# Spacing the row gathers of a four-layer kernel: one weight piece behind each gather in the expert layer, paced gathers and loads in linear attention

## What is computed

```python
x = L0_attn_x
x = _layernorm(x + _L0_attn_ref(x))     # dilated attention on every second row
x = _layernorm(x + _L0_ffn_ref(x, ...)) # switch layer: each row through its best of 8 experts
x = _layernorm(x + _L1_attn_ref(x, W))  # linear attention
x = _layernorm(x + _L1_ffn_ref(x, ...)) # soft mixture: dispatch to 64x32 slots, combine
```

```python
# switch layer, for each expert e; w1[e] is 256 x 2048, w2[e] is 1024 x 256
a, g = jnp.split(x @ w1[e], 2, axis=1)
y = jax.nn.silu(a) * g @ w2[e]
out = jnp.where((max_ind == e)[:, None], y, out)   # then out * max_prob
# linear attention
q, k, v = jnp.split(x @ W, 3, axis=-1)
q, k = elu(q) + 1, elu(k) + 1
V = einsum('bld,bhd,bl->blh', q, einsum('bld,blh->bhd', k, v), 1 / (q . k.sum + EPS))
```

## Time and profile before

| | us |
|---|---|
| median of 3 runs | 1529.8 |
| lowest, highest | 1528.87, 1532.9 |
| profiled execution, its own time | 1531.05 |
| span in the profile (first to last instruction) | 1529.2 |
| outside the span | 1.85 |

### The profile page before, as it was taken

The page is one execution under the profiler, slowest core; times in us unless marked ns, Lnnn a source line. Parts: engine busy times, 40 slices in busy tenths (PEclk is TensorE's granted clock), DMA queues, the critical chain, the costliest instruction groups (busy, mean ns, idle before and its releaser), DMA issues. The chain is left out here.

```text
span 1529.2 us, 27827 instructions
## 1 busy us (share of the span) xinstructions
PE 1380.1 (90%) x8930; PEld 1202.3 (79%) x8931; DVE 885.1 (58%) x1768; ACT 612.1 (40%) x1077; POOL 680.1 (44%) x546
## 2 busy tenths in 40 slices
PE   6997387999999994599978999999999997999997
PEld 3444276888888883477768999999999987999997
DVE  4788612222222223377559877877877853666655
ACT  3554322333333331377643323323323315555553
POOL 6663087776670003411006655655655652540500
PEclk9998688999999997699989999999999998999999
DMA  4112334222220003500023263653653657365350
GB/s 158 45 45 70 124 96 135 97 96 96 96 96 14 14 15 111 195 1 1 1 83 97 84 174 88 178 168 90 179 168 88 179 175 283 129 233 198 137 203 38
DMA packets 109194, 171.17 MB, mean 112 GB/s; under 512 B 6128, under 2 KB 95088, under 8 KB 101712
## 3 DMA queue, kind: packets, MB, share of 16 engines
q1 hardware_dynamic: 100112, 156.00, 31.5%
q0 software_dynamic: 3408, 9.31, 2.1%
q10 hardware_dynamic: 5616, 5.11, 1.0%
HBM read 114.96 MB, written 55.44 MB: 111 GB/s over the span
## 5 line engine op out<-in xcount | busy, mean ns | idle before, releaser
L1572 PE MATMUL disp_psS<-disp_e,last_x 128*128 128x256 f32 x1024 | 233.1, 381 | 3.6 <-POOL disp_e L1659 3.6
L1572 PEld LDWEIGHTS disp_psS<-disp_e,last_x 128*128 128x128 f32 x1024 | 191.2, 191 | 28.2 <-POOL disp_e L1659 4.2
L1557 PE MATMUL disp_psL<-phi_hold,hand_xh 128*128 (+1 forms) x1024 | 200.3, 296 | 4.9 <-DVE disp_e L1724 4.8
L1666 POOL TENSOR_TENSOR disp_s<-disp_e 128x512 f32<-128x512 f32 x64 | 82.3, 1286 | 263.9 <-ACT disp_e L1642 263.9
L1845 PE MATMUL comb_psO<-phi_hold,comb_eh 128*128 (+1 forms) x1024 | 198.2, 291 | 0.4 <-DVE comb_el L1943 0.4
L1557 PEld LDWEIGHTS disp_psL<-phi_hold,hand_xh 128*128 128x128 f32 x1024 | 165.4, 194 | 8.9 <-issue 5.9
L1624 ACT ACTIVATE disp_raw<-disp_psL 128x512 f32<-128x512 f32 x128 | 76.4, 597 | 220.9 <-PE disp_psL L1557 156.4
L1845 PEld LDWEIGHTS comb_psO<-phi_hold,comb_eh 128*128 128x128 f32 x1024 | 156.8, 189 | 0.9 <-DVE comb_el L1943 0.8
L1659 POOL TENSOR_TENSOR disp_e<-disp_e,disp_rs 128x1024 f32<-128x1024 f32 x64 | 151.6, 2369 | 0.0
L1557 PE MATMUL disp_psL<-phi_hold 128*128 (+1 forms) x512 | 145.8, 285 | 0.0
L1845 PE MATMUL comb_psO<-phi_hold,comb_el 128*128 (+1 forms) x512 | 144.1, 281 | 0.0
(11 more groups left out here) (258 smaller groups left out, 3116.1 us busy)
## 6 DMA issues: line engine op xcount, KB each, us to landing
logits<-disp_raw SPq DMA_DIRECT2D x64, 512.0 KB, 4.1
hand_e<-logits SPq DMA_DIRECT2D x32, 1024.0 KB, 6.7
w_raw<-in_w SPq DMA_DIRECT2D x8, 2048.0 KB
disp_wt<-in_w_slot SPq DMA_DIRECT2D x16, 1024.0 KB, 8.0
w_raw<-in_w SPq DMA_DIRECT2D x8, 1024.0 KB
disp_bt<-in_b_slot SPq DMA_DIRECT2D x8, 1024.0 KB, 11.2
slot_y<-disp_yb SPq DMA_DIRECT2D x60, 128.0 KB, 3.2
comb_y_in<-slot_y SPq DMA_DIRECT2D x3, 2048.0 KB, 10.6
```

The costliest lines, as they stand in the source:

```text
L1557: last = nc.tensor.matmul(psL[p][:, b, :], xp[:, kd, t * P:(t + 1) * P], pp[:, kd, bass.ds(k * BLK, BLK)], start=b % 2 == 0 and kd == 0 an ...
L1572: last = nc.tensor.matmul(psS[kd][:, b, :], x[:, b * TB + mc, kd * P:(kd + 1) * P], e[mc % 4][:, b, :], start=mc == 0 and b % 2 == 0, stop ...
L1666: nc.gpsimd.tensor_tensor(s2[:], e[mc % 4][:, 0:2, :], e[mc % 4][:, 2:4, :], ALU.add).then_inc(pair_sum, 1)
```

## The change

In the switch layer the low part of expert 1 is cut into 32 pieces in place of 12: w1's 4096 columns into 16 pieces of 256, w2's 2048 columns into 16 pieces of 128. The loop around it is the same, so one piece now stands behind each gather of slots 3 to 34, and the last four gathers have nothing between them. The semaphore counts stay: `split` goes up by 2 behind the last piece of w1 and by 2 behind the last of w2.

In linear attention the gathers of tiles 0 to 15 stay as they were. Gather t of tiles 16 to 31 waits for `k_raw` to reach t - 15, which is when tile t - 16 has been projected. The first eight low parts of phi stand between gathers 23 and 24, the other eight behind gather 31. On SP, phi's load waits for `k_raw` 2, the load of x of batch 2 for `k_raw` 6, and that of batch 3 for `k_raw` 14.

```diff
-    CHUNK = 512
-    LOW_CHUNKS = (KD * 2 * FF + FK * D) // CHUNK
+    CHUNKS = 16
+    LOW_CHUNKS = 2 * CHUNKS
     def low_chunk(self, pool, e, n):
-        first = KD * 2 * FF // self.CHUNK
-        part, at = (0, n) if n < first else (1, n - first)
+        first = self.CHUNKS
+        part, at = divmod(n, self.CHUNKS)
         _, raw, hi, lo = self.parts()[part]
-        cols = slice(at * self.CHUNK, (at + 1) * self.CHUNK)
+        size = (KD * 2 * FF, FK * D)[part] // self.CHUNKS
+        cols = slice(at * size, (at + 1) * size)
...
             for b in range(B):
-                if b == 2:
-                    sp.dma_start(phi[:], phi_dram.rearrange("(k p) n s -> p k (n s)", p=P)).then_inc(phi_loaded, 16)
                 if b == 1:
                     sp.wait_ge(gathered[TB - 1], 16)
+                if b == 2:
+                    sp.wait_ge(k_raw, 2)
+                    sp.dma_start(phi[:], phi_dram.rearrange("(k p) n s -> p k (n s)", p=P)).then_inc(phi_loaded, 16)
+                if b > 1:
+                    sp.wait_ge(k_raw, (b - 2) * TB + TB - 2)
                 sp.dma_start(x[:, b * TB:(b + 1) * TB, :], rows[:, b * TB:(b + 1) * TB, :]).then_inc(x_loaded[b], 16)
         @block.gpsimd
         def _(pool):
-            for t in range(NT):
+            def fetch(t):
+                wait(pool, k_raw, t - 2 * TB + 1)
                 nc.gpsimd.indirect_dma_start(yg[:, t, :], None, ys_dram, ...
-            for i in range(PARTS):
+
+            def low_part(i):
                 j = i // PARTS_PER_ROW
                 cols = slice(i * PC, (i + 1) * PC)
                 pool.wait_ge(o_raw, j + 1)
                 pool.wait_ge(phi_high, i // (PARTS // KD) + 1)
                 nc.gpsimd.tensor_tensor(lo_flat[:, cols], ...
+
+            for t in range(2 * TB):
+                fetch(t)
+            for b in range(2, B):
+                for t in range(b * TB, (b + 1) * TB):
+                    fetch(t)
+                for i in range((b - 2) * TB, (b - 1) * TB):
+                    low_part(i)
```

## The result

| | before | after |
|---|---|---|
| median of the runs side by side | 1531.08 us | 1505.89 us |
| span in the profile | 1529.2 us | 1502.7 us |

What follows compares the result with a forecast made beforehand. The prediction took PE to bound the kernel, with time to win only where dense POOL gathers stopped it. Gains of 11.0 (switch layer) and 15.5 us (linear attention) made 26.5 off 1529.8: forecast 1503.5 us, range 1499 to 1517.

Steps and rivals of the forecast that it cites:

- PE's holes at 249 and 619 us: Switch layer and linear attention: PE busy only 4.4 of 13 us and 6.5 of 19 us, where time could be won.
- Part 1, the stop: Switch layer, tiles 4 to 15: spacing the gathers 1.86, then 1.58 us apart removes the stop, worth 13.0 us.
- A: Rival: the switch layer's stop stays because gathers 1.6 to 1.9 us apart are too dense; 1514.3 us, chance 0.15 with halves.
- L: Rival: the switch layer's stop stays because the loop's first turn causes it; 1514.3 us, chance 0.05.
- Who stood still: Both stops: ACT stood still first, with waits of 18.6 and 11.6 us that nothing in the engines' records released.
- Part 1, what gets later: Switch layer's expert loads: expert 2 in time by 1 us, PE waits 2 us for expert 3, leaving 11.0 us gained.
- the duration of expert 2's first load: Switch layer: 7.75 us from expert 3's rows, plus 0.7 for four gathers beside it; w1 ready at 273.6.
- Part 2: Linear attention: pacing gathers and loads removes a 16.0 us stop, less 0.5 for phi's load, gaining 15.5 us.
- The model by batch 1's rows: Linear attention, batch 0: without a stop, `lin_kv` follows the second tile's keys by 20.5 us, as in batch 1.
- rival B: Linear attention's stop stays, from sixteen back-to-back gathers with 1 MB of x, or phi's load; 1519 us, chance 0.05.
- what counts is how densely POOL issues gathers: Both stops: gathers 1.25 us apart for long enough stop ACT and slow PE; 2.4 us apart cost nothing.
- Rival C: Both layers: neither stop goes, since bytes in flight count, not spacing; about 1530 us, chance 0.05.

Runs made afterwards that it cites:

- Session C: Follow-up session on another chip without stops, kernel before 1505.4 us: halves of linear attention's pacing, moved burst and thin gathers, each beside the kernel before.
- A: Session of the main result: the whole change against the kernel before, 1505.89 us against 1531.08, ratio 0.9844.
- D: Follow-up session on a chip without stops: the whole change against the kernel before, 1505.31 us against 1505.95, ratio 0.9997; also a moved-burst run.
- the near-zero gap: Kernel before plus a one-column POOL memset (0.1 us) behind each gather of slots 0 to 2 and 15 to 38; 1523.84 us.
- the paced gathers of session C: Kernel before with only linear attention's gathers 16 to 31 paced, loads and switch layer as before; 1505.83 us, ratio 1.0003.
- E: Follow-up session without stops: changed kernel with the next expert's w1 loaded earlier, 1500.86 us against the kernel before's 1505.26; also a moved-burst run.
- B: Follow-up session with stops, kernel before 1530.6 us: switch-layer change only 1521.48 us, linear-attention change only 1512.70, changed kernel with earlier w1 load 1501.22.

## Why the prediction was right, and where it was not

**What stands.** PE's holes at 249 and 619 us were the place of the gain. Each part removed its own stop, and the parts add up (9.1 and 17.9 us alone). Why dense gathers hold PE, and why on some chips or in some sessions only, stays open (below).

**Part 1, the stop.** Forecast: 13.0 us. Gate product 7 comes 13.3 us earlier than before (284.51 to 271.19). Spacing of 1.6 to 1.9 us was enough; the row could not tell, since the choice was made between two ends, and luck has a share in that. Rivals A and L (0.20 together) fell with it. Session C speaks once more against L: the loop's first turn is there, the stop is not.

**Who stood still.** The prediction says that ACT stood still first and that its waits were released by nothing. That reading is wrong: ACT waited for semaphores of PE, raised 16.1 and 15.5 us late (above). The forecast didn't hang on it, since it priced the whole hole and tied it to the gathers. (A small slip beside it: ACT's stop is in step 5, not 6, since the copy at 261.44 is that of tile 3.)

**Part 1, what gets later.** This term was mis-sized. Forecast: expert 2 in time by 1 us, expert 3 late by 2 us. Measured: PE waited at both, and tiles 8 and 11 cost 3.8 and 1.7 us more than in the steady pace. The step that failed is the duration of expert 2's first load. I took 7.75 us from expert 3's rows and added 0.7 for four gathers beside it; it took 10.9 us, with the last gathers and a store beside it (the second weight's 1 MB stood behind expert 3's load too). The loads of 7.6 to 7.8 us without gathers and 10.2 us with them, in the experiments above, point to the gathers. The margin that I had left was 1 us, and w1 was ready 3.1 us later than forecast, at 276.7. A second thing wasn't priced, the clock: at tile 8

```profile
276.90 0.49 PE L922 MATMUL moe_psH<-w_hi,moe_xh 128*128 x1 [1.97 <-POOL w_lo L826]
```

PE waited 2.0 us, and the other 1.8 us are slow matmuls: the granted clock from 278 to 284 us is 0.73, and at 0.50 of it a matmul comes each 0.43 us in place of 0.23. The layer gave 7.7 us up to tile 19 in place of 11. Another 1.5 us came between tile 19 and linear attention. That is not the change: the stretch takes about 194.3 us in some profiles and 195.6 to 195.9 in others, of the same kernel too (the changed one 194.3 in A, 195.7 in D), with no visible cause.

**Part 2.** Forecast: 15.5 us, 16.0 less 0.5 for phi. Measured in the profile: 16.4, and phi was there. The model by batch 1's rows was right to 0.1 us (20.5 and 20.5). One number in the argument against rival B was wrong: behind gather 7 stand 5 MB of loads, not 4 (x of three batches and phi); at its 7.75 us for 2 MB they end at 627, and in the trace they end near 630, still ahead of 637.42.

**The sum** was 26.5 us of span, forecast and measured. That the two agree so closely is luck: the 3.3 us that part 1 gave too little came back as 0.9 in part 2, the 1.5 between the layers that the change didn't cause, and 0.9 of small differences at the start and the end. By the medians it was 25.2.

**What was not foreseen.** The step "what counts is how densely POOL issues gathers" is true only in half. Density is needed: the near-zero gap keeps the stop at 1.25 us, the change loses it at 1.6. It isn't enough: on three chips the same density stops nothing. Something that differs from chip to chip, or from session to session, comes in, and no run here shows what it is.

Three things can be said against guesses. It isn't the program or its data: they are the same. Nor do instruction blocks come late on the queues that the trace records: in the kernel before, blocks are moved at 235 and 244 us, ahead of the stop, and at 615 in linear attention, much as with the paced gathers of session C, at 235, 247 and 606. And what comes late in a stop are first of all semaphores of matmuls that PE had already been through by the profile, which a wait for new instructions would not explain by itself; this is argued, not tested. The Trainium skill, Runtime: NRT & Kernel Launch, section Instruction fetch mechanics, has fetches mostly hidden. The traces of C to E agree, in so far as no semaphore of PE is over 0.02 us late and ACT has no wait put down to "remote"; those of A and B don't show whether the stop has to do with fetching.

One more difference is in the traces, and it leaves a rival untested. Those of A and B lack some 440 to 820 of about 10,280 records of raised semaphores, most of all where the gathers run and most in the kernel before; those of C to E lack hardly any. The stop may come from whatever loses these records, or from the recording itself. Every run here gives its span and clock, so no time is known of an execution that wasn't recorded.

Rival C of the prediction ("neither goes, 1530") was the nearest to a flat outcome, but not its reason: what I never priced is that there might be no stop to remove.

## What to carry to other kernels

An engine that waits for something "remote" may be waiting for its neighbour's late semaphore: look at the engine that should raise it. Read such a stop as a property of that execution until a second chip shows it; run the kernel before beside each experiment, and look at its time first. Long rows of back-to-back indirect DMAs on GpSimd are worth spacing with other work, here to 1.6 us or more apart: it made no measurable difference where nothing stops (ratio 0.9997), and saved 25 us where something does. When a stall is removed, what it covered comes due: re-time the chain behind it (here loads and divisions of weights, 5.5 us) from the changed start, and ask of each load what runs beside it.

## What the runs showed of the hardware that was not expected

- The same kernel takes 1531 us in sessions A and B and 1505 us on the three other chips of C to E, each time stable (all runs of a session within 0.6%). The difference is two stops, worth 13 and 16 us, during bursts of indirect DMAs 1.25 us apart; the same bursts are in the traces of C to E, and no stop.
- In the switch layer's stop PE isn't halted but crawls: 10 matmuls in 13 us without a semaphore between them, where 78 ran on a chip without stops. Its semaphores come up to 17.7 us behind the matmuls that raise them; those of ACT, VectorE and POOL do not.
- A 2 MB load took 7.8 us from issue to use with its 1 MB neighbour behind it, and 10.9 us with four gathers of 128 KB and a store beside it.
- In one run a tile took 9.43 us in place of 9.53, with the same instructions of PE and the switch layer's buffers moved by 156 bytes in each partition. Whether the move is the reason wasn't tested.
